# Attention and routed feed-forward on one core: V turned by VectorE, three banks of maxima in every attention step, lambda's chain moved

## What is computed

```python
xn = _layernorm(x, axis=-1)
x = x + _L0_attn_ref(xn, ...) + _L0_ffn_ref(xn, ...)
# attention: 8 heads, two score maps each (16 subheads of depth 8), values of depth 16
q = _apply_rope(q, freqs, scale); k = _apply_rope(k, freqs, 1.0 / scale)
probs = softmax(q @ k.T)
lam = exp(sum(lambda_q1 * lambda_k1)) - exp(sum(lambda_q2 * lambda_k2)) + LAMBDA_INIT
diff = probs[:, :, 0] - lam * probs[:, :, 1]
attn = diff @ v;  attn = attn * rsqrt(mean(attn * attn) + 1e-05) * (1 - LAMBDA_INIT);  return attn @ Wo.T
# feed-forward: a router picks 3 of 8 zones for each batch
top_p, top_i = top_k(softmax(tanh(mean(x) @ W1 + b1) @ W2 + b2), 3)
out = x + sum over the picked zones e of w[e] * (gelu(x @ Wa[e]) @ Wb[e])
```

## Time and profile before

| | |
|---|---|
| time, median of 3 runs | 429.36 us (429.24 to 430.72) |
| the profiled execution's own time | 429.37 us |
| its span | 427.6 us |
| PE busy | 412.2 us (96%) |
| DVE busy | 383.8 us (90%) |
| ACT busy | 344.1 us (80%) |
| POOL busy | 146.1 us (34%) |

### The profile page before, as it was taken

One profiled execution on the slowest core, in us unless ns is written; L12 is line 12 of the kernel. 1 busy time (PEld: TensorE's weight loads), 2 busy tenths in 40 slices (PEclk: granted clock), 3 DMA queues, 4 the chain that ended last, 5 costly groups with the idle time before them and its releaser, 6 DMA issues.

```text
span 427.6 us, 7728 instructions
## 1 busy us (share of the span) xinstructions
PE 412.2 (96%) x2750; PEld 191.0 (45%) x2750; DVE 383.8 (90%) x737; ACT 344.1 (80%) x459; POOL 146.1 (34%) x179
## 2 busy tenths in 40 slices
PE   8998999999999999999999999999999999999996
PEld 6664566566665333333333333333333333335544
DVE  4989999999999899999999999999999999888575
ACT  2787765675654799889899989989999999989993
POOL 4159998988863500111020110120103303420000
PEclk9999999999999999999999999999999999999999
DMA  9726760400000060020002054000000000000003
GB/s 268 304 92 208 264 231 22 138 13 1 3 0 2 16 233 2 4 98 4 2 1 101 1 129 71 3 2 2 3 2 2 3 0 3 2 3 2 2 2 100
DMA packets 21872, 24.95 MB, mean 58 GB/s; under 512 B 11818, under 2 KB 16106, under 8 KB 21578
## 3 DMA queue, kind: packets, MB, share of 16 engines
q1 hardware_dynamic: 21096, 23.60, 17.5%
q10 hardware_dynamic: 738, 0.86, 0.8%
HBM read 14.49 MB, written 8.65 MB: 54 GB/s over the span
## 4 chain that ended last, share of the span: by engine, by line
PE 74%; DVE 11%; ACT 7%; issue 5%; DMA 1%; POOL 1%; ACTq 0%
PE ps L1395 21%; PE ps L1358 16%; PE ps L1248 13%; ACT E L809 6%; DVE part_max L924 6%; PE ps L1320 4%; PE ps L1173 3%; PE ps L1175 3%; PE ps L1174 3%; PE ps L1386 3%; PE ps L1321 2%; PE ps L1322 2%; PE ps L1376 2%; DMA X<-in_x 1%; PE ps L1350 1%
## 5 line engine op out<-in xcount | busy, mean ns | idle before, releaser
L924 DVE TENSOR_REDUCE part_max<-ps 128x1 f32<-128x512 f32 x512 | 320.6, 681 | 21.9 <-PE ps L1248 15.0
L809 ACT ACTIVATE E<-ps 128x1024 f32<-128x1024 f32 x256 | 245.3, 1029 | 29.3 <-PE ps L1358 25.9
L1395 PE MATMUL ps<-E,Vg 128*32 128x512 f32 x896 | 119.3, 604 | 0.0
L1248 PE MATMUL ps<-K,Q 32*128 32x512 f32 x384 | 104.2, 463 | 1.4 <-DVE part_max L924 1.1
L1358 PE MATMUL ps<-Q,K 32*128 32x512 f32 x320 | 70.8, 489 | 2.1 <-ACT E L809 1.4
L559 POOL TENSOR_TENSOR hL<-h,hH 128x512 fp32r<-128x512 f32 x48 | 61.4, 1288 | 13.1 <-ACT hH L769 11.2
L1358 PEld LDWEIGHTS ps<-Q,K 32*128 32x128 f32 x320 | 28.6, 181 | 82.7 <-ACT E L809 72.3
L767 ACT ACTIVATE h<-ps 128x512 f32<-128x512 f32 x48 | 28.8, 601 | 33.6 <-PE ps L1175 25.1
L1248 PEld LDWEIGHTS ps<-K,Q 32*128 32x128 f32 x384 | 44.4, 182 | 23.9 <-DVE part_max L924 19.3
L610 POOL TENSOR_TENSOR U<-AT,rsum 128x256 f32<-128x256 f32 x15 | 9.3, 623 | 102.4 <-DVE rsum L1060 102.4
L1248 PE MATMUL ps<-xnL,xnH 32*128 32x512 f32 x128 | 41.8, 454 | 0.9 <-DVE part_max L924 0.7
(11 more groups left out here) (171 smaller groups left out, 418.0 us busy)
## 6 DMA issues: line engine op xcount, KB each, us to landing
K<-k_scr SPq DMA_DIRECT2D x5, 512.0 KB, 3.8
Q<-q_scr SPq DMA_DIRECT2D x5, 512.0 KB, 7.1
tab<-in_tables SPq DMA_DIRECT2D x2, 1024.0 KB, 10.0
wa_raw<-in_wa SPq DMA_DIRECT2D x6, 256.0 KB, 2.9
wb_raw<-in_wb SPq DMA_DIRECT2D x6, 256.0 KB, 3.2
Q<-max_turned SPq DMA_DIRECT2D x80, 2.0 KB
X<-in_x SPq DMA_DIRECT2D x2, 512.0 KB, 7.0
k_scr<-V SPq DMA_DIRECT2D x2, 512.0 KB, 10.9
```

The source lines that it names most:

```text
L809: nc.scalar.activation(E[:, par, 2 * jj:2 * jj + 2, :].rearrange("p j t -> p (j t)"), ps[:, 2 * jj:2 * jj + 2, :].rearrange("p j t -> p (j ...
L924: nc.vector.tensor_reduce(part_max[:, tile // FC % 2, j * FC + tile % FC, sh:sh + 1], ps[:, SLOT_BANK[x], :], AX.X, ALU.max).then_inc(slot ...
L1248: mm(ps[:, SLOT_BANK[x], :], Qs[g % KQ_BUFS][strip(j), tile % TB * P:(tile % TB + 1) * P], Ks[g % KQ_BUFS][strip(j), sh * BANK:(sh + 1) * ...
L1395: last = mm(ps[QUAD * j:QUAD * (j + 1), B_PV, :], Vg[:, par, st, j // 2, :], E[:, s % 2, k, :], start=(st == 0), stop=(st == TB - 1), skip ...
```

## The change

- **V.** PE's 16 transposes and ACT's 16 copies go. ACT copies each chunk once to zT (`values_turn` of ACT), DVE transposes it in 32x32 blocks to vB (two chunks ahead of feed-forward, two in its units 5 and 13, `VALUES_AT`), and SP puts the blocks in place by 16 transfers of 64 KB in pieces of 128 bytes. POOL's `v_group` now sets Vg to one (the first two times) and copies the values alone.
- **Lambda.** The chain of 12 instructions leaves the place ahead of feed-forward and goes into attention steps 13, 29, 45 and 61, three in each (`LAMBDA_AT`).
- **Maxima.** Every attention step from 1 to 120 makes three banks; step 0 makes 4 as before. In the first 16 tiles the order of halves changes (`quad`).
- **Loads.** x's first half, w_in, the constants, x's second half now follow each other on SP's queue; the small loads come first on ACT's queue and the strips' selector last. POOL's fill of V is a quarter as long.
- **POOL and PE in the opening.** `rope_low(1)` waits for `pick_done`; `rope_low(2)` and `rope_low(3)` go into feed-forward units 0 and 1, `wa_zone(1)` to unit 3, `ADD_AT` and `LOW_AT` three units later. `strip_rows(2)` and `(3)` go behind `second(1)` and `second(2)`.

The core of the diff:

```diff
-MAX_STEPS, PACE_STEPS = 121, 98
+MAX_STEPS = 121
+def quad(t):
+    return (t % FC, t // FC) if t < TB else (t // 2, t % 2)
 def max_slots(s):
-    own = GJ * 2 * TB
     def up_to(n):
-        if n <= PACE_STEPS:
-            return GJ * LEAD - (-n * (GJ * (QUADS - LEAD) - own) // PACE_STEPS)
-        return GJ * QUADS - own + min(own, -(-(n - PACE_STEPS) * own // (MAX_STEPS - PACE_STEPS)))
+        return min(GJ * LEAD + (3 * n + 1 if n else 0), GJ * QUADS)
+LAMBDA_AT = (13, 29, 45, 61)
-ADD_AT, LOW_AT = (3, 4), (6, 8)
+ADD_AT, LOW_AT = (6, 7), (9, 11)
+VALUES_AT = (5, 13)
...
# SP
+            x_load(0)
+            sp.dma_start(w_in[:], wqkv).then_inc(w_arr, 16)
+            sp.dma_start(cst[:], consts).then_inc(c_in, 16)
+            x_load(1)
...
             raw_next(2)
+            sp.wait_ge(vb_done, CHUNKS)
+            for a in range(GB):
+                for q in range(P // QUAD):
+                    rows, feats = slice(QUAD * q, QUAD * (q + 1)), slice(QUAD * a, QUAD * (a + 1))
+                    sp.dma_start(V1[rows, 2 * SEQ:].rearrange("p (n j) -> p n j", j=P)[:, :, feats],
+                                 vB[feats, :].rearrange("p (n q j) -> p n q j", n=TILES, q=P // QUAD)[:, :, q, :]).then_inc(v_in, 16)
             max_rows(0)
...
# POOL
             rope_low(0)
+            pool.wait_ge(pick_done, 2)
             rope_low(1)
             rope_add(2)
             rope_add(3)
-            rope_low(2)
             wa_zone(0)
-            rope_low(3)
             wb_zone_low(0)
             for n in range(UNITS):
                 h_low(n)
-                if n == 1:
+                if n < 2:
+                    rope_low(2 + n)
+                if n == 3:
                     wa_zone(1)
...
# DVE
-            lambdas()
+            def values_turn(c):
+                dve.wait_ge(vt_done, c + 1)
+                if c == 0:
+                    dve.wait_ge(rope_done, 4)
+                nc.vector.transpose(vB[:, c * BANK:(c + 1) * BANK], zT[:, c * BANK:(c + 1) * BANK]).then_inc(vb_done, 1)
+            values_turn(0)
+            values_turn(1)
...
+                if s in LAMBDA_AT:
+                    lambdas(LAMBDA_AT.index(s))
```

More of the change, by code:

```diff
@@ L178 @@
 PROJ_BANK = ((4, 5), (6, 0), (1, 4), (5, 6), (4, 5), (4, 5))
-STRIP_BANK = (0, 0, 7, 1)
+STRIP_BANK = (0, 0, 1, 1)
 V_BANK = (2, 3, 2, 3)
-ADD_AT, LOW_AT = (3, 4), (6, 8)
+ADD_AT, LOW_AT = (6, 7), (9, 11)
+V_LOADS = GB * (P // QUAD)
+VALUES_AT = (5, 13)
 def proj_bank(k):
@@ L248, in build @@
         (Vg,), r3b = region(r2, ("Vg", [P, 2, TB, 2, QUAD], F32))
-        (wa_raw, wb_raw, waH, waL, wb_f, wbH, wbL, h, hH, hL, rot, vT), r4 = region(
+        (wa_raw, wb_raw, waH, waL, wb_f, wbH, wbL, h, hH, hL, rot), r4 = region(
             r3, ("wa_raw", [P, 2, FF], F32), ("wb_raw", [P, 2, FF], F32),
@@ L340, in _, with x_load @@
         def _(sp):
-            for b in range(BATCH):
+            def x_load(b):
                 sp.dma_start(X[:, b * TB:(b + 1) * TB, :],
                              x[b * SEQ:(b + 1) * SEQ, :].rearrange("(n p) d -> p n d", p=P)).then_inc(x_in[b], 16)
+            x_load(0)
+            sp.dma_start(w_in[:], wqkv).then_inc(w_arr, 16)
+            sp.dma_start(cst[:], consts).then_inc(c_in, 16)
+            x_load(1)
             for kind in range(2):
@@ L711, in values_turn @@
                 act.wait_ge(vt_ps, c + 1)
[L712 to L722, removed]
+                nc.scalar.activation(zT[:, c * BANK:(c + 1) * BANK], ps[:, V_BANK[c], :], ACT.Copy).then_inc(vt_done, 1)
             act.wait_ge(c_in, 16)
@@ L1046, in _, with lambdas @@
                     reduce_slot(t, k)
+                if n in VALUES_AT:
+                    values_turn(2 + VALUES_AT.index(n))
                 if n >= UNITS - 2:
                     rotary(EARLY // 2, (n - (UNITS - 2),))
+            def lambdas(part):
+                nl, ab, cc, c2, nlc = (lt[:, k:k + 1] for k in range(5))
+                if part == 0:
+                    dve.wait_ge(lam_exp, 1)
+                    link(nc.vector.scalar_tensor_tensor(nl, lam_e[:, 1:2], LAMBDA_INIT, lam_e[:, 0:1],
+                                                        ALU.subtract, ALU.subtract))
+                    link(nc.vector.tensor_scalar(ab, nl, -1.0, None, ALU.mult))
+                    link(nc.vector.tensor_tensor(ab, ab, nl, ALU.max))
+                elif part == 1:
+                    link(nc.vector.tensor_scalar(ab, ab, 1.0, None, ALU.add))
+                    link(nc.vector.reciprocal(cc, ab))
+                    link(nc.vector.tensor_scalar(cc, cc, LAMBDA_RANGE, 1.0, ALU.mult, ALU.min))
+                elif part == 2:
+                    link(nc.vector.tensor_tensor(c2, cc, cc, ALU.mult))
+                    link(nc.vector.tensor_scalar(epsc[:], c2, EPS, SQRT_LEAST, ALU.mult, ALU.max))
+                    link(nc.vector.tensor_scalar(limit[:], c2, FLT_MAX, None, ALU.mult))
+                else:
+                    link(nc.vector.tensor_tensor(nlc, nl, cc, ALU.mult))
+                    link(nc.vector.tensor_scalar(comb[:], cst[:, C_E0:C_E0 + 2 * QUAD], cc, None, ALU.mult))
+                    nc.vector.scalar_tensor_tensor(comb[:], cst[:, C_E1:C_E1 + 2 * QUAD], nlc, comb[:],
+                                                   ALU.mult, ALU.add).then_inc(comb_done, 1)
             def query_rows(a, th, part):
@@ L1212, in values @@
                 if c >= 2:
-                    pe.wait_ge(v_out, c - 1)
+                    pe.wait_ge(vt_done, c - 1)
                 t = slice(c * BANK, (c + 1) * BANK)
                 three(ps[:, V_BANK[c], :], wH[:, 4, :], wL[:, 4, :], xnH[:, t], xnL[:, t], True, True).then_inc(vt_ps, 1)
-            def values_turn(c):
-                pe.wait_ge(vt_done, c + 1)
-                for k in range(FC):
-                    last = nc.tensor.transpose(ps[:, V_BANK[c], k * P:(k + 1) * P], vT[:, c % 2, k * P:(k + 1) * P], ident)
-                last.then_inc(v_done, 1)
             def ring_free(x):
@@ L1278, in _ @@
             project(7)
-            values_turn(0)
-            values_turn(1)
+            values(2)
+            values(3)
             strip_rows(1)
-            values(2)
             pe.wait_ge(wsel, 1)
@@ L1287, in _ @@
             last.then_inc(wb_ps, 1)
-            pe.wait_ge(rot_done, 5)
+            project(8)
             max_slot(0, 0)
             max_slot(0, 1)
-            values(3)
-            project(8)
             project(9)
-            values_turn(2)
-            values_turn(3)
+            project(10)
+            project(11)
             max_slot(0, 2)
             max_slot(0, 3)
-            project(10)
-            project(11)
-            pe.wait_ge(wbc_done, 1)
-            strip_rows(2)
             def chunk(n):
```

81 lines of the change are left out of this document (30 added, 51 removed).

## The result

The changed kernel takes 436.76 us (median of 4 executions, 435.48 to 438.89) beside 430.04 us for the kernel before (429.24 to 431.05): the ratio is 1.0151, 95% interval [1.0121, 1.0182]. It is slower, outside the range of 422.5 to 427.7. The profiled execution took 438.89 us with a span of 437.1 us and a mean granted clock of PE of 0.979 (1.00 stands for 2.4 GHz, 0.50 for 1.2 GHz), where the one before had 427.6 us and 1.00; it is the slowest of the four, so its trace holds about 2 us more than the median.

The account below looks back on a forecast made before the run. No engine had room to spare; PE set feed-forward's pace before, POOL would after the change. 429.37 us less 2.5 for opening and feed-forward and 2.0 for attention gives 424.9 us, range 422.5 to 427.7.

Parts of the forecast that it names:

- The opening: Start of the kernel: x's first half lands earlier, second four transposes no longer wait for ACT; 0.4 us gained, between 0 and 0.5.
- PE starts no earlier than 11.6: Opening: PE's warm-up runs until 11.59 us, so x's earlier landing cannot bring PE's start ahead of 11.6.
- Rival (c): Opening's lead lost, `h_low(0)` at 36 or later because ACT or the selector's load is late; only attention gains, 427.4; chance 0.08.
- The router's stall: Router's choice: the second of two DVE stalls beside POOL's ropeL, about 1.04 us, goes; 0.5 us gained for `wsel`.
- the layout: Opening behind `wsel`: engines' queues laid out by traced durations, putting `h_low(0)` at 33.7 us against 36.78 before.
- Feed-forward: POOL instead of DVE holds PE; `second(15)` no earlier than 69.3 against 71.80, opening and feed-forward together gaining 2.5 us.
- POOL without idle time up to unit 14: Feed-forward sign: POOL works without a gap, 33.1 us from the start of `h_low(0)` to the end of `h_low(14)`.
- The last full half's rows: Attention: last bank comes some 3.3 us later, of 4.4 us 1.1 are left for landing; nothing added, 0.7 in the range.
- rival (b): Attention: the four-bank steps' stalls come back elsewhere, mean step stays at 258.97 / 121, time 426.9; chance 0.15.
- 21-step stretch: Attention, 318.77 to 362.84 us: 21 steps of 2.10 us each, said to contain one four-bank step; used against the returning stalls.
- rival (e): Slower: lambda's chain stalls in attention as before, 6.9 us holding DVE; fully paid 431.0 us; chance 0.05.
- the 0.7 that I had in the sum: Attention: each of three quarters' transposes, in steps 106, 111 and 116, costs 0.7 us as in step 104; 2.1 us together.

Follow-up runs that it names:

- the selector's copy moved: The changed kernel, strips still loaded last, with ACT's copy of the selector behind the normalisation of all of X instead of ahead of the first root: 432.12 us, ratio 1.0028.
- the last one: The changed kernel with the old pace of maxima, POOL's rotary work later, lambda in steps 103 to 114, selector's copy behind X's normalisation: 429.12 us, ratio 0.9966.
- strips-and-pace: The changed kernel with the strips' load first on ACT's queue and the pace of maxima of the kernel before: 430.94 us, ratio 1.0006.
- later rotary work: strips-and-pace with POOL's rotary additions moved from units 6 and 7 to 15 and 16, splits from 9 and 11 to 17 and 19: 429.31 us, ratio 0.9983.
- three banks alone: The kernel before with only the edit to three banks of maxima in every step: 432.69 us, ratio 1.0055.
- the strips' load: The changed kernel with ACT's load of the selector strips put back ahead of its six small loads: 432.69 us, ratio 1.0042.
- the pace: The changed kernel with the kernel before's pace of maxima (four banks in steps 16, 32, 49, 65 and 81): 434.27 us, ratio 1.009.
- lambda in feed-forward: strips-and-pace with lambda's four parts in units 1 to 4 of feed-forward instead of attention steps 13, 29, 45 and 61: 431.98 us, ratio 1.0054.

## Why the prediction was wrong

**The opening** was forecast 0.4 us earlier; it was 3.06 late. The step that failed is "PE starts no earlier than 11.6": I took this lower bound, argued from PE's warm-up and X, as the time of the start, and did not read ACT's order (selector's copy, then root) against the strips' new place: PE waited 3.91 us and started at 14.87. Rival (c) named the selector's load, but let it only cancel a lead and gave it 0.08. The router's stall went as argued: its two instructions take 0.79 and 0.21 us now, for 0.78 and 1.25 before, and the last one, which now runs beside the moved `rope_low(1)`, 0.70 for 0.22. From the first transposes to `h_low(0)` it takes 34.38 - 11.29 = 23.09 us with the selector's copy moved, and 36.78 - 11.81 = 24.97 before: 1.9 us won, where the layout had 33.7 - 11.4 = 22.3, or 2.7. So `h_low(0)` comes at 34.1 to 34.9 in the kernels in which the wait is undone, and not at 33.7; only in the last one, where the transposes start at 10.46, it comes at 33.55.

**Feed-forward** was to keep 2.5 us. From `h_low(0)` to `second(15)` I laid out 35.6 us, and it took 36.8 both in the changed kernel and in strips-and-pace. The step that failed is "POOL without idle time up to unit 14": two calls of `strip_rows` of 0.86 us on PE inside units 1 and 2 had no price in the sum; then ACT waits for PE, and POOL for ACT. The view of waits of the changed kernel from 43.8 to 76.5 us has all three:

```profile
ACT h L778 <- POOL hL L582: 10.0, 12, 1.4
...
ACT h L778 <- PE ps L1199: 1.4, 1, 1.4
...
POOL hL L582 <- ACT hH L780: 1.1, 1, 1.1
```

In strips-and-pace `h_low(14)` ends at 68.1, 34.0 us behind the start of `h_low(0)`, where I had laid out 33.1: POOL's 1.05 us of idle time makes most of the 1.2 us. That it comes from the strips is read from this order of waits; no run moved `strip_rows` back. That POOL binds several units was right. ACT's 10.0 us of waiting for `h_low` does not show it by itself, since the kernel before has 8.1 us from unit 1 to 15 and its PE kept its pace; the later rotary work shows it, with 1.1 us.

The transposes in units 5 and 13 cost 0.5 us together, if all that units 6 and 14 are longer is theirs, and V's 16 transfers, issued from 74.91 to 85.73 us, were hidden, as said. Of the 2.89 us that feed-forward loses against before, 1.09 lie behind unit 15, where the granted clock is 0.91 in 130 to 150 us.

**Attention up to step 82** was right in kind. Steps 16, 32, 49, 65 and 81 lost their stalls, worth 2.60 us (three banks alone), so rival (b) falls, though not by its "21-step stretch": steps 82 to 103 hold none of the four-bank steps. Lambda cost 174.46 - 173.03 = 1.43 us, where I took 0.8 from a range of 0 to 2.3. Its instructions did not stall, as rival (e) would have it: 0.13 to 0.28 us each.

**The last full half's rows** are the second failed step. I let its scores come behind step 103's products and left 4.4 us from the end of issue to the need. In the trace of after they come behind step 102's, about 2.2 us sooner; that leaves 2.2 us, and the landing takes 1.1 of it (issue ended at 367.37, PE went on at 368.49). A delay of 3.3 then gives 2.2 us of wait, which is what all five kernels with three banks in every step show. All five have a granted clock of 0.89 in 350 to 380 us, and all the others 1.00. So the clock added to it, although no rows are missing any more: steps 103 to 108 take 13.20 us for 11.14. The last 0.63 us, in steps 108 to 121 (28.76 for 28.13), are not the clock's: they fall at 1.00, and the step with the third quarter's transpose takes 2.81 us (398.12 to 400.93) for 2.08 before, the 0.7 that I had in the sum. Together 4.9 us.

**The sum.** In profiled executions: opening and its clock +2.9, feed-forward up to step 0 +2.9, attention -1.2 and +4.9, together 9.5; by the medians it is 6.7. By single edits (differences of the ratios times 430) 5.3 us come back by the selector's copy or 4.7 by the strips' load, and 2.6 by the pace; both together (strips first and old pace) give 6.2. Undoing the wait gives more than the 2.5 us that the order of the loads cost the kernel before. Of this the starts explain 0.5 to 0.9 us: without the wait the transposes come at 11.29 and 10.93, ahead of the 11.81 before. The rest is not settled, as the intervals of these differences are over 1 us wide. The one rival for "slower" was lambda's stall, and none had a tile that comes late: I had weighed the engines' busy time, and not what stands behind the instruction that waits.

**Open.** The clock also fell in the profiled execution of the changed kernel in 33 to 37 us (0.57) and in 130 to 150 us, and in some of the other kernels at about these places, in others not, with nearly the same busy time of PE (18.5 to 18.8 of 20 us in 130 to 150). Executions of one kernel differ in it too. Why one and not the other was not settled. Whether tables or X's second half kept the strips back for 8.1 us was not tried either.

## What to carry to other kernels

Before a load is moved back, read what stands behind the instruction that waits for it, on its own engine: here a copy made at 11.63 us, whose first reader came at 27.09, stood ahead of the root that everybody needed. Moving the waiting instruction is then as good as moving the load. And when a producer's pace is evened out, look for the latest consumer that lived from the old pace: two steps of delay in one half cost twice what five removed stalls gave.

## What the runs showed of the hardware

One and the same idle time of PE was paid twice: 2.18 us of waiting for the rows, and then 2.1 us over the next five steps, of which the eight matmuls of 1.94 us instead of 1.06 are the visible part. With a wait of 0.7 us at the same place the clock stayed at 1.00, and the same five steps took 11.40 us for 11.14. In the opening the projections' matmuls behind a wait of 3.91 us took 0.63 us instead of 0.39, and with 12 more matmuls on zeros over the same time they did not.

Beside POOL some small DVE instructions last until POOL's instruction ends. The tensor-tensor on 128x1 that takes 0.14 to 0.16 us in the changed kernel's attention took, with lambda in feed-forward, 1.07 us beside POOL's `h_low` and ended with it (47.54 and 47.52); the two on 128x64, a tensor-scalar with its factor in SBUF and a scalar-tensor-tensor, took 1.24 and 1.22 us where they take 0.26 and 0.28 in attention. The tensor-scalar with constants, in the same units, took 0.15 us, and the reductions from PSUM were not touched. The Trainium skill (SBUF — State Buffer, "Who interferes with whom") says that a DVE instruction with two inputs in SBUF contends with a GpSimd instruction that reads SBUF, that tensor-scalar can do so in a two-port mode, and that the one issued later blocks: the trace agrees in these rows for the instructions with two inputs. The held tensor-scalars fit the second part (the one of 1.24 us here, and the router's first of 0.78 in the earlier trace rows, to which the rule on two inputs does not apply), but no row shows an instruction's mode.
